# Maxima's scores between a step's first two exponent products, a normalisation on ScalarE, and slabs at other steps

## What is computed

```
y = layer_norm(x);  q = y @ q_w + q_b;  k = ctx @ k_w + k_b;  v = ctx @ v_w + v_b
scores = q k^T / sqrt(32), masked;  out = softmax(scores) v
h = out @ cproj_w + cproj_b + x
result = h + gelu(layer_norm(h) @ fc_w + fc_b) @ proj_w + proj_b      # inner width 2048
```

## Time and profile before

| | us |
|---|---|
| median of 3 runs (785.68 to 788.26) | 787.35 |
| the profiled execution: its time, its span | 787.93, 786.1 |
| TensorE busy | 754.0 (96%) |
| VectorE, GpSimd, ScalarE busy | 466.1, 290.8, 275.4 |

### The profile page before, as it was taken

The page is one execution under the profiler, slowest core; times in us unless marked ns, Lnnn a source line. Parts: engine busy times, 40 slices in busy tenths (PEclk is TensorE's granted clock), DMA queues, the critical chain, the costliest instruction groups (busy, mean ns, idle before and its releaser), DMA issues.

```text
span 786.1 us, 10028 instructions
## 1 busy us (share of the span) xinstructions
PE 754.0 (96%) x3664; PEld 516.6 (66%) x3664; DVE 466.1 (59%) x1008; ACT 275.4 (35%) x489; POOL 290.8 (37%) x171
## 2 busy tenths in 40 slices
PE   7999999989899999998999999999999999999998
PEld 5878886633334434343434888888888888888886
DVE  6673337779988789889695767643422433322213
ACT  4434241356765656665575101111112111211111
POOL 2644040056787676699576101122002200130000
PEclk9999999979999999999999999999999999999999
DMA  9656387596666576478631436421120403030001
GB/s 321 229 160 235 115 247 222 190 274 157 174 157 141 148 194 173 123 194 178 166 121 54 162 106 180 129 98 64 32 75 1 161 13 84 12 107 1 1 1 53
DMA packets 94385, 103.25 MB, mean 131 GB/s; under 512 B 39968, under 2 KB 48420, under 8 KB 94336
## 3 DMA queue, kind: packets, MB, share of 16 engines
q1 hardware_dynamic: 94192, 102.59, 45.7%
q10 hardware_dynamic: 144, 0.02, 0.0%
HBM read 73.08 MB, written 29.37 MB: 130 GB/s over the span
## 4 chain that ended last, share of the span: by engine, by line
PE 80%; DVE 10%; ACT 4%; POOL 3%; issue 2%; DMA 0%; SPq 0%; POOLq 0%; DVEq 0%; ACTq 0%
PE ps L474 22%; PE ps L476 21%; PE ps L475 21%; DVE ps L983 6%; PE ps L597 5%; PE ps L581 5%; PE ps L566 3%; ACT Pt L774 3%; PE ps L612 2%; POOL RAWY L1276 1%; PE ps L534 1%; POOL R L1276 1%; DVE R L919 1%; POOL R L1214 1%; DVE mx L983 1%
## 5 line engine op out<-in xcount | busy, mean ns | idle before, releaser
L774 ACT ACTIVATE Pt<-ps 128x512 f32<-128x512 f32 x256 | 134.0, 603 | 86.2 <-PE ps L581 83.8
L1146 DVE CAST HR<-R 128x512 fp32r<-128x512 f32 x52 | 24.5, 471 | 185.3 <-ACT R L809 185.3
L809 ACT ACTIVATE R<-ps,cols 128x512 f32<-128x512 f32 x52 | 35.9, 690 | 227.2 <-PE ps L476 227.1
L581 PE MATMUL ps<-BIG 98*128 98x512 f32 x256 | 94.9, 449 | 15.9 <-ACT Pt L774 12.3
L581 PEld LDWEIGHTS ps<-BIG 98*128 98x128 f32 x256 | 45.1, 191 | 87.9 <-ACT Pt L774 37.7
L983 DVE CUSTOM_DVE_ANT_0 ps<-ps,FU 128x512 f32<-128x512 f32 x128 | 84.4, 720 | 19.2 <-PE ps L566 19.2
L983 DVE CUSTOM_DVE_ANT_0 ps<-ps,BIG 128x512 f32<-128x512 f32 x128 | 84.4, 721 | 16.0 <-PE ps L566 15.9
L474 PE MATMUL ps<-YT,BIG 128*128 128x512 f32 x192 | 74.9, 390 | 0.0
L475 PE MATMUL ps<-YT,BIG 128*128 128x512 f32 x192 | 74.7, 389 | 0.0
L476 PE MATMUL ps<-YT,BIG 128*128 128x512 f32 x192 | 74.7, 389 | 0.0
L474 PE MATMUL ps<-BIG,HR 128*128 128x512 f32 x192 | 74.7, 389 | 0.0
(11 more groups left out here) (127 smaller groups left out, 1376.8 us busy)
## 6 DMA issues: line engine op xcount, KB each, us to landing
BIG<-qs SPq DMA_DIRECT2D x62, 256.0 KB, 2.8
BIG<-ks SPq DMA_DIRECT2D x62, 256.0 KB, 3.1
ks<-BIG SPq DMA_DIRECT2D x32, 256.0 KB, 2.0
qs<-BIG SPq DMA_DIRECT2D x32, 256.0 KB, 6.1
R<-hd SPq DMA_DIRECT2D x28, 256.0 KB, 3.9
R<-in_x SPq DMA_DIRECT2D x16, 256.0 KB, 4.5
hd<-R SPq DMA_DIRECT2D x16, 256.0 KB, 2.0
yt<-FU SPq DMA_DIRECT2D x64, 64.0 KB, 1.9
```

Of the source, the lines that this page charges most:

```text
L581: eng.matmul(bk, K_[0:98, j, kc * 128:(kc + 1) * 128], Q_[0:98, j, :], start=True, stop=True).then_inc(S["p_ra"], 1)
L774: eng.activation(Pt[:, r, j % 2, :], bank(bank_a(("s2", i, j))), ACT.Exp, scale=SCALE).then_inc(S["a_ra"], 1)
L809: eng.activation(g, bank(4 + i % 2), ACT.Gelu_apprx_tanh, bias=fcb[:, f:f + 1]).then_inc(S["a_g"], 1)
L1146: eng.tensor_copy(HR[:, n, 0, :], g).then_inc(S["v_hh"], 1)
```

## The change

In steps 0 to 55 with kc < 3, `s1` stands behind `s2(i,0)`, and `s2(i,1)`, the transpose and `pv` behind `s1`; from step 56 on (kc < 3) `pv` stands between `s2(i,0)` and `s2(i,1)`. The rings keep their order. The second layer norm of sequence 0 (`HN`) is normalised by ScalarE at steps 45, 47, 49 and 51, with scale `rs` and a bias `nb` = -mean x `rs` that VectorE makes at step 45. ScalarE evicts the last query whole into `HN` and rounds it from there; GpSimd makes the low part, and the bank is free after ScalarE's first instruction (`a_qb`). Slabs 0 and 1 are split in steps 56 to 58, slab 2 by VectorE in feed-forward step 0. `y_affine` runs in step 56. Loads of slabs 2, 3 and 4 follow their buffers.

```diff
-        Y_BLOCKS, Y_AFFINE, Y_HIGH, Y_LOW = (48, 49, 52, 53), (57, 57, 57, 57), (57, 57, 58, 58), (58, 58, 59, 59)
+        Y_NORM, Y_BLOCKS, Y_AFFINE = (45, 47, 49, 51), (48, 49, 52, 53), (56, 56, 56, 56)
+        Y_HIGH, Y_LOW = (57, 57, 58, 58), (58, 58, 59, 59)
...
-        SLAB_HIGH, SLAB_LOW = (59, 60, 62), (60, 61, 63)
+        SLAB_HIGH, SLAB_LOW = (56, 57), (57, 58)
...                                                        # TensorE, a step of the loop
                 if kc < 3:
                     s2(i, 0)
+                if i in GROUPS:
+                    s1(GROUPS[i])
+                if i >= 2 and (kc == 3 or i not in GROUPS):
+                    pv(i - 2)
+                if kc < 3:
                     s2(i, 1)
                 if i in TURNS:
                     turn_maxima(TURNS[i])
-                if i in GROUPS:
-                    s1(GROUPS[i])
-                if i >= 2:
+                if i >= 2 and kc < 3 and i in GROUPS:
                     pv(i - 2)
...                                                        # ScalarE, qk_high
+                if (b, g, which) == (*LAST_Q, 1):
+                    eng.activation(HN[:, 0, :], bank(proj_bank(u)), ACT.Identity, bias=vec[:, 2, g:g + 1]).then_inc(S["a_qb"], 1)
+                    act.wait_ge("a_qb", 1)
+                    eng.activation(QK[n][:, 0, :], HN[:, 0, :], ACT.Copy).then_inc(S["a_qh"], 1)
+                    return
...                                                        # ScalarE, a step of the loop
+                if i in Y_NORM:
+                    c = Y_NORM.index(i)
+                    act.wait_ge("v_nb", 1)
+                    eng.activation(HN[:, c, :], HN[:, c, :], ACT.Identity, bias=nb[:, c:c + 1],
+                                   scale=rs[:, 0, c:c + 1]).then_inc(S["a_nm"], 1)
...                                                        # VectorE
-                if i == 1:
-                    qk_low(*LAST_Q, 1)
...
+                if i == 45:
+                    dve.wait_ge("g_rs", 5)
+                    eng.scalar_tensor_tensor(out=nb[:, :], in0=mv[:, 0, :, 0], scalar=-1.0, in1=rs[:, 0, :],
+                                             op0=ALU.mult, op1=ALU.mult).then_inc(S["v_nb"], 1)
...                                                        # VectorE, feed-forward step 0
                 if i == 0:
+                    slab_high(2)
+                    slab_low(2)
                     divide_a(NS - 1)
...                                                        # GpSimd
+                if i == 1:
+                    pool.wait_ge("a_qh", 32)
+                    low(QK[3][:, 1, :], HN[:, 0, :], QK[3][:, 0, :], "g_ql")
...
-                if i in (44, 46, 48, 50):
-                    c = (i - 44) // 2
-                    pool.wait_ge("g_rs", 5)
-                    eng.tensor_scalar(HN[:, c, :], HN[:, c, :], mv[:, 0, c, 0:1], rs[:, 0, c:c + 1],
-                                      ALU.subtract, ALU.mult).then_inc(S["g_nm"], 1)
```

More of the change, by code:

```diff
@@ L57, in cross_attention_block @@
         ve = sb("ve", [128, 2, 4], F32)
+        nb = sb("nb", [128, 4], F32)
         mh = sb("mh", [128, 4], F32)
@@ L134, in cross_attention_block @@
                      "p_pj", "p_tr", "p_ra", "p_rb", "p_pv", "p_sm", "p_cp", "p_fc", "p_pr",
-                     "a_hi", "a_v", "a_qh", "a_xh", "a_ra", "a_pv", "a_ab", "a_ah", "a_wc", "a_g",
+                     "a_hi", "a_v", "a_qh", "a_qb", "a_nm", "a_xh", "a_ra", "a_pv", "a_ab", "a_ah", "a_wc", "a_g",
                      "v_hi", "v_lo", "v_bn", "v_ag", "v_ve", "v_nm", "v_yb", "v_ya", "v_mf", "v_fu", "v_ql", "v_rb", "v_t1", "v_rc",
                      "v_t2", "a_sh", "v_at", "v_wc", "v_ac", "v_sh", "v_sl", "v_hh", "v_hl", "v_o", "v_cp",
-                     "g_rs", "g_nm", "g_lo", "g_xl", "g_ac", "g_al", "g_xc", "g_sl", "g_hb",
+                     "g_rs", "g_lo", "g_xl", "g_ac", "g_al", "g_xc", "g_sl", "g_hb", "g_ql", "v_nb",
                      "d_vec", "d_m8", "d_mk", "d_on", "d_cb", "d_pb", "d_wc", "d_m"):
@@ L163, in evicted @@
             b, n = divmod(u, 12)
+            if u == 47:
+                return "a_qb", 1
             return ("a_v", 4 * b + n + 1) if n < 4 else ("v_ql", 8 * b + n - 3)
@@ L227, in lows @@
         def lows(f):
-            return ("g_sl", 2 * f + 2) if f < 3 else ("v_sl", 2 * f - 4)
+            return ("g_sl", 2 * f + 2) if f < 2 else ("v_sl", 2 * f - 2)
         def stacked(s):
@@ L256, in store_qk @@
                 scr = (ks, qs)[which]
-                for h, done in ((0, "a_qh"), (1, "v_ql")):
-                    sp.wait_ge(done, kq + 1)
+                for h, done in ((0, ("a_qh", kq + 1)), (1, ("v_ql", kq + 1) if (b, g, which) != (*LAST_Q, 1) else ("g_ql", 1))):
+                    sp.wait_ge(*done)
                     eng.dma_start(scr[4 * b + g, h].rearrange("j d t -> (j d) t"),
@@ L320, in ln2_load @@
                     sp.wait_ge("p_pj", 48)
+                    sp.wait_ge("g_ql", 1)
                 elif b == 1:
@@ L812, in slab_high @@
                 act.wait_ge(f"d_w{f % 2}", 32 * (f // 2 + 1))
[L813 to L816, removed]
+                act.wait_ge("p_ra", last_s2(13))
                 for h in range(2):
@@ L923, in y_block @@
                 if b == 0:
-                    dve.wait_ge("g_nm", c + 1)
+                    dve.wait_ge("a_nm", c + 1)
                 else:
@@ L1012, in slab_low @@
                 for h in range(2):
-                    dve.wait_ge("v_sh", 2 * f + h - 5)
+                    dve.wait_ge("v_sh", 2 * f + h - 3)
                     eng.tensor_tensor(sl[2 * h + 1], RW[:, f % 2, 512 * h:512 * h + 512], sl[2 * h].bitcast(F32),
@@ L1019, in slab_high @@
                 dve.wait_ge(f"d_w{n}", 32 * (f // 2 + 1))
-                if f == 3:
+                if f < 4:
                     dve.wait_ge("p_rb", RB[("s1", 16 * NS - 1)] + 1)
-                    dve.wait_ge("g_al", 14)
-                    dve.wait_ge("v_at", NS)
+                    if f == 3:
+                        dve.wait_ge("g_al", 14)
+                        dve.wait_ge("v_at", NS)
                 elif f < 6:
```

## The result

The changed kernel takes 784.1 us (median of 20 runs, 779.7 to 787.02) against 788.18 (20 runs, 785.3 to 789.85): a ratio of 0.9949 with the 95% interval 0.9931 to 0.9966, 4.1 us less. Forecast were 777.8 and a range from 771.5 to 783.5, so the direction held and the size did not. The clock that TensorE is granted dips at different places from run to run, and the runs of one program spread with it over some 7 us (779.7 to 780.26 in the three runs of the changed kernel with a mean clock of 0.999, 785.36 to 786.69 in the five at 0.989); where little time is at stake I therefore compare stretches of the traces between two fixed instructions, not medians. One run of an experiment at 934.06 us and one of the kernel before at 1458.59 us, both in a slow state, are left out of all medians.

A forecast was written before the change was run, and what follows sets the result against it. TensorE was taken to bound the kernel (80% of the chain). Fill 3.8, normalisation 2.0 and tail 4.9, less 1.1 for the third slab, make 9.6 us off 787.35: 777.8 us, range 771.5 to 783.5.

The forecast's parts named there:

- The fill: Attention loop, steps 4 to 55: the new order fills TensorE's hole, saving 0.29 us per four-step period, 3.8 us in all.
- D: Fourth interval between maxima groups in a four-step period, 5.22 us: group waits only for its bank, net -0.52.
- B: Second interval between maxima groups, 4.44 us: score 1 leaves the way, 0.63 less; extra product adds 0.43, net -0.20.
- C: Third interval between maxima groups, 3.81 us: no hole to fill, so it grows by 0.43.
- The extra product: Attention loop: score 1 placed between maxima group and weighted sums costs TensorE 0.43 us, bounds 0.23 and 0.50.
- cheap product: Rival: the extra score costs 0.23 us, the clock holds at the end, the third slab hides; 770.6 us, chance 0.17.
- The normalisation: Steps 48 to 51: relieving GpSimd removes the long VectorE product and the period's whole excess, 2.0 us (1.0 to 2.0).
- The tail: Steps 56 to 63: slab casts 3.1 us, Y's affine step 1.0, clock 0.8; together 4.9 us less (3.1 to 5.8).
- The clock: Fall of TensorE's clock at 418 us: 1.7 us would come back at full clock; half taken, 0.8.
- The third slab: Feed-forward part: VectorE's casts and subtractions delay the second gelu's split, a new stall of 1.1 us (0 to 2.0).
- dear product and thin tail: Rival: extra product 0.50 us, Y's loads late, clock falls again, collision costs half; up to 782.4 us, chance 0.22.
- the hole only moves: Rival: score 1 waits for VectorE, new TensorE waits in 42 steps; 787 (chance 0.07) or slower, 798.8 (0.07).

The follow-up runs named there:

- the additions moved: Changed kernel with GpSimd's bias additions of residual quarters 0 and 2 moved from kc = 2 to kc = 0 steps: 782.58 us, ratio 0.9945.
- the tail alone: Kernel before with only slabs 0 and 1 split in steps 56 to 58, slab 2 by VectorE, Y's affine steps in step 56: 785.56 us, ratio 0.9979.
- the double additions: Changed kernel with more GpSimd bias additions in kc = 2 steps, quarters 1 and 2 together in one step: 783.97 us, ratio 0.995.
- the version with both changes: Changed kernel with GpSimd's bias additions moved to kc = 0 steps and the third slab split behind the last division: 779.66 us, ratio 0.9909.

## Why the prediction was wrong

**The fill: the step that failed.** "The three without pieces have no piece to wait for, so D gains more and B less; I count them alike. 13 x 0.29 = 3.8 us." The intervals were taken from one period, which has no `x_add`, and multiplied by 13. In that kind of period they held: A 3.27, B 4.30, C 4.24, D 4.80, so 16.61 in place of 16.77, a gain of 0.16 where 0.29 was due (B and D came out 0.06 and 0.10 longer; D's part is the signal, for which 0.04 was allowed without a row: the piece's addition ends at 268.49, the group starts at 268.64, 0.15 later). But of the nine marked periods five have an addition, and there D is 5.36, the period 17.16, a loss of 0.39. Old order against new in the same kernel: 151.16 to 152.25, +1.09 us, where the nine had -2.6. With the additions moved the order is worth -1.65 in the nine (149.51). The prediction had the mechanism in hand: of the periods with the same additions it said that "none of them is long". That served to put the whole excess of steps 48 to 51 on the normalisations; that the same meeting would count once D is shorter was not asked. It was harmless because TensorE's order left about half a microsecond in D, and that half microsecond was what the change removed. Ahead of step 19 the clock falls in every profile, but not always in the same steps. At full clock the copies of the maxima of steps 4, 8, 12 and 16 stand 14.62, 14.62 and 15.48 apart with the new order (an addition in the last) and 14.76, 14.91 and 15.29 with the old: 0.24 less in three periods. What the order does in steps 0 to 3 stays open.

**The extra product.** 0.43 was right: C is 4.24 as predicted, and B 4.30. The cheap product (0.23) is refuted by both; the dear one (0.50) would suit B (4.31) but not C (4.31).

**The normalisation.** -2.0 predicted, -1.86 (old order against before) and -2.09 (alone) found. The price of the eviction of the last query, nothing, agrees with its run to within 1.7 us.

**The tail.** The affine step gave the 1.0 that it was given. Three slab pairs at 1.03 each, 3.1 us, was mis-sized: a term was counted whole because ScalarE had no idle time there, and only the last pair stood in front of TensorE's wait; 1.67 came back. The new order in steps 56 to 63 was no term at all: 17.60 + 17.55 with the old order, 16.22 + 17.66 with the new one, so -1.27. These two errors nearly cancel.

**The clock.** 0.8 was half of a fall. None of the eight profiled kernels with the slabs moved has a fall between 414 and 424 us, and of the five with the old tail four have one. None of 76 runs of the kernel before has a mean clock over 0.998; 11 of 88 runs of kernels with the slabs moved have 0.999 or 1.0. But it is not the slabs alone: the new order alone, with the old tail, has 1.0 in 2 of its 12 runs, and the tail alone, with the slabs moved, in none of 12. And over all of them the mean is 0.9931 against 0.9925, which is 0.3 us (a line through the 76 runs of before gives 0.46 us for a thousandth of clock), no more than the uncertainty of the means. Falls at 159 to 223 us outweigh it. The prediction named "a clock below 1.0 inside the loop" as a sign of error; the changed kernel's profile has it twice (183 to 197, 217 to 221 us), but before has such falls too.

**The third slab.** +1.1 predicted; a wait of 1.01 where it was placed, and 1.3 over the whole feed-forward part.

The sum of what was found: +1.1 (order, nine periods), -0.2 (order, steps 4 to 15), -2.0 (normalisation), -1.7 (slabs), -1.0 (affine), -1.3 (order in the tail), -0.3 (clock), +1.3 (third slab) is -4.1, against a measured -4.1. So close an agreement is chance, as the measured one lies between 2.7 and 5.4 by its interval, and the profiles that the terms come from differ in clock. Of the shortfall of 5.5 us against 9.6 the fill is 4.7, of which the collisions are five times 0.55, 2.75, and 0.3 in steps 12 to 15; the slabs are 1.4, the clock 0.5, the third slab 0.2, and the order in the tail gave 1.3 back. The rival "dear product and thin tail" came nearest (782.4), but that was luck: of its four reasons only the clock's came true, in part; "the hole only moves" was nearer in spirit, as a new wait did take the place of the old one, but on VectorE and in one interval of four.

## What to carry to other kernels

When a reordering shortens an interval that one engine sets, look at the second engine in every instance of that interval, not in one: what is late there without consequence today becomes the bound. That some cost shows no effect in a profile says only that there is slack to hide it, so ask whether the change spends that slack. Work taken off an engine is worth mostly what stood directly ahead of another engine's wait (1.04 of the 1.67 here); read the remaining idle time behind each piece before counting all of them.

## What the runs showed of the hardware

A VectorE product of two tensors in memory (0.68 us alone) that meets a GpSimd addition does not run slower in proportion: it ends about 0.55 us behind the end of the GpSimd instruction it met, whether it started 0.12 or 0.68 us after that one. The Trainium skill ("SBUF — State Buffer", SBUF: two separate sides) says that the pair of ports is held for a whole instruction; the double additions agree, as the product had its turn between them. The 3.26 us of the earlier trace rows do not fit as well: there the product was passed over once, an addition that followed a pair sum went first. In the same trace, at 343.74, the product met a pair sum with an addition behind it and had its turn between the two (1.17 us, and the addition took 1.74). Why the two cases differ, no run here settles.

The same pause of TensorE in the same steps of two executions was followed by a fall of the clock in one and not in the other. Windows of 2 us, the changed kernel first, then the version with both changes: start and end, length, TensorE's busy time and count, granted clock, busy share of the DMA engines, GB/s:

```profile
158.00:160.00 2.00, 0.63 (x6) 1.00 1.06 347
160.00:162.00 2.00, 2.00 (x14) 1.00 1.07 218
162.00:164.00 2.00, 1.31 (x10) 1.00 1.07 239
```

```profile
158.00:160.00 2.00, 0.71 (x2) 1.00 1.08 384
160.00:162.00 2.00, 1.92 (x9) 0.54 1.06 213
162.00:164.00 2.00, 2.00 (x10) 0.50 1.07 236
```

TensorE paused in both at 158 to 160, 1.16 us ahead of the same group of maxima; one kept the full clock (2.4 GHz), the other was granted the lower level (1.2 GHz) behind it. I had read a fall in one profile as a property of the kernel; it is a chance that differs from run to run, and a gain of one or two microseconds has to be looked for between fixed instructions outside the falls.
